# Landmark attention and the norm behind it in one stage, in a two-layer decoder on one core

## The reference, cut to what matters

```python
x = x + landmark(layernorm(x))            # L0_attn
x = x + heads(layernorm(x), ctx)          # L0_xattn: causal self and cross attention, 16 heads of 16
x = x + fp6_linear(layernorm(x))          # L0_ffn
x = x + hyperbolic(layernorm(x))          # L1_attn
x = x + two_mha_blocks(layernorm(x), ctx) # L1_xattn
x = x + experts(layernorm(x))             # L1_ffn, top 2 of 8

def landmark(x):                          # x: (4, 512, 256)
    q = softmax(x @ Wq + bq); k = softmax(x @ Wk + bk); v = x @ Wv + bv   # over all 256 features
    kl = k.reshape(B, 64, 8, 256).mean(axis=2)                            # 64 landmarks
    mid = (kl @ k.T) @ (k * v)                                            # (64, 256)
    return (q @ kl.T) @ mid
```

## Time and profile before

| | |
|---|---|
| median of 3 runs | 4048.33 us (4047.57 to 4056.62) |
| the profiled execution's own time | 4053.46 us |
| its span, first to last instruction | 4051.7 us |
| PE, DVE, ACT, POOL busy, share of the span | 83%, 51%, 40%, 23% |
| mean granted TensorE clock | 0.925 of full |

### The profile page before, as it was taken

How to read it: one execution, slowest core, us unless ns; L and a number is a source line. 1 busy time by engine, 2 the same in 40 slices (tenths; PEclk the granted TensorE clock), 3 DMA queues, 4 the chain that set the end, 5 groups by cost and what they waited for, 6 DMA issues and landing times. The chain is left out here.

```text
span 4051.7 us, 56156 instructions
## 1 busy us (share of the span) xinstructions
PE 3359.0 (83%) x21550; PEld 1837.2 (45%) x21550; DVE 2079.9 (51%) x4231; ACT 1633.4 (40%) x2349; POOL 919.6 (23%) x961
## 2 busy tenths in 40 slices
PE   6887788988887788988887888988876888947997
PEld 4325545254334535254234543263254452436886
DVE  5655665634655665634746555535656556430111
ACT  3353833333445642433437542433538333411221
POOL 1202822011105522012116420012018220140111
PEclk9998799999997898999997998999997999958998
DMA  4102012011202022011220121012120121134554
GB/s 116 55 13 78 1 45 89 20 38 45 59 24 55 1 49 84 20 43 40 59 69 11 32 71 51 19 24 60 38 78 1 45 72 37 35 126 159 172 180 150
DMA packets 227190, 239.73 MB, mean 59 GB/s; under 512 B 95542, under 2 KB 193956, under 8 KB 224612
## 3 DMA queue, kind: packets, MB, share of 16 engines
q1 hardware_dynamic: 219552, 215.73, 18.3%
q10 hardware_dynamic: 3620, 10.07, 0.7%
q0 software_dynamic: 3744, 10.26, 0.7%
HBM read 167.24 MB, written 68.76 MB: 58 GB/s over the span
## 5 line engine op out<-in xcount | busy, mean ns | idle before, releaser
L867 ACT ACTIVATE prob<-psum 128x1024 f32<-128x1024 f32 x384 | 372.2, 1021 | 509.0 <-PE psum L785 509.0
L1235 ACT ACTIVATE prob<-psum 128x1024 f32<-128x1024 f32 (+3 forms) x384 | 331.6, 914 | 363.8 <-PE psum L1136 363.8
L913 DVE TENSOR_REDUCE scr<-psum 128x1 f32<-128x512 f32 x576 | 369.0, 685 | 195.9 <-PE psum L772 192.1
L1275 DVE TENSOR_REDUCE stats<-psum 128x1 f32<-128x512 f32 (+3 forms) x576 | 331.9, 619 | 140.9 <-PE psum L1124 137.7
L782 PE MATMUL psum<-stack 32*128 32x512 f32 x1536 | 226.5, 660 | 15.2 <-ACT prob L867 10.4
L398 PE MATMUL psum<-ident 128*128 128x128 f32 x1704 | 213.5, 280 | 0.0
L398 PEld LDWEIGHTS psum<-ident 128*128 128x128 f32 x1704 | 203.7, 195 | 14.9 <-issue 13.8
L1124 PE MATMUL psum<-stack 96*128 96x512 bf16 (+3 forms) x576 | 181.8, 364 | 31.5 <-DVE stats L1275 31.1
L815 PE MATMUL psum<-prob,ones_f 128*32 128x512 f32 x1536 | 202.1, 594 | 0.0
L1151 PE MATMUL psum<-prob,vbig 128*32 128x512 f32 (+3 forms) x1536 | 189.4, 566 | 4.2 <-ACT prob L1235 4.2
L2832 PE MATMUL psum<-xgT,ew 128*128 128x256 f32 x736 | 167.8, 387 | 18.0 <-DVE xgT L2880 18.0
(11 more groups left out here) (483 smaller groups left out, 6495.9 us busy)
## 6 DMA issues: line engine op xcount, KB each, us to landing
ew<-in_L_ffn_W SPq DMA_DIRECT2D x46, 1024.0 KB, 7.8
stack<-q_terms SPq DMA_DIRECT2D x144, 128.0 KB, 2.5
w_mlp<-in_L_xattn_a_li_w SPq DMA_DIRECT2D x16, 1024.0 KB, 6.2
q_terms<-parts SPq DMA_DIRECT2D x96, 128.0 KB, 2.2
stack<-k_terms SPq DMA_DIRECT2D x72, 128.0 KB, 2.9
stack<-k_terms SPq DMA_DIRECT2D x36, 256.0 KB, 4.4
w_mlp<-a_terms SPq DMA_DIRECT2D x36, 256.0 KB, 4.7
a_keys<-stack SPq DMA_DIRECT2D x4, 2048.0 KB, 6.3
```

The costliest lines, as they stand in the source:

```text
L867: act.activation(prob[:, i % 4, :, :], psum[:, 2 * p:2 * p + 2, :], ACT.Exp, scale=scale).then_inc(exped, 1)
L913: dve.tensor_reduce(found[:, c:c + 1], ring(i), AX.X, ALU.max).then_inc(freed, 1)
L1235: act.activation(prob[:, i % 4, :, q0:T], psum[:, 2 * p:2 * p + 2, q0:T], ACT.Exp, scale=scale).then_inc(exped, 1)
L1275: dve.tensor_reduce(found[:, c:c + 1], ring(i)[:, 0:keys_of(t)], AX.X, ALU.max).then_inc(freed, 1)
```

## The change

Four things are edited:

1. **Stores.** The stores of u2 count on a semaphore `rows_out` of the kernel instead of one of the stage, and nobody waits for them in u2. SP waits for them in the next batch's front (and, after the loop, in a small stage named "after"). PE runs four idle matmuls at the end of u2.
2. **Context norm.** The transposes of the normed context and ACT's write of `cnT` move from the end of front into Asm, behind the last products. PE runs four idle matmuls at the end of front.
3. **Asm by halves.** Maxima, exponentials, and divisions are done for tiles 0 and 1, then 2 and 3. Six keys are made ahead of the transposes, one behind the landmarks and one behind `mid`; k2 comes before k1.
4. **n2 gone.** The late values and the norm, by halves, are in Asm.

```diff
@@ mlp_unit, SP
                 for t in range(QT):
                     sp.wait_ge(done, t + 1)
-                    storing(sp, t).then_inc(stored, 16)
-                sp.wait_ge(stored, 16 * QT)
+                    storing(sp, t).then_inc(e.rows_out, 16)
@@ mlp_unit, PE, at the end when final is None
+                e.keep_running(pe, 4, 0)
@@ beginning
+        @block.sync
+        def _(sp):
+            sp.wait_ge(e.rows_out, 16 * QT)
...
-            pe.wait_ge(raw_in, 1)
-            pe.wait_ge(cn_made, CT)
-            for t in range(CT):
-                last = pe.transpose(psum[:, 6 + t // 4, t % 4 * P:(t % 4 + 1) * P], cn[:, t, :], ident[:, :])
-            last.then_inc(cn_turned, 1)
+            e.keep_running(pe, 4, 1)
...
-            act.wait_ge(cn_turned, 1)
-            act.activation(cnT.rearrange("p k (a n) -> p (k a) n", n=BANK), psum[:, 6:8, :], ACT.Identity,
-                           bias=affine[1][:, 0:1], scale=affine[0][:, 0:1])
@@ landmark_attention, DVE
+            for h in range(2):
+                for t in HALVES[h]:
+                    ins = dve.tensor_reduce(mxq[:, 2 * t:2 * t + 2],
...
+            take_key(0)
+            divide(0)
+            take_key(1)
+            divide(1)
+            take_key(4)
+            take_key(5)
+            dve.wait_ge(lm, 1)
+            dve.tensor_copy(klT, psum[:, 7, 0:KT * L].rearrange("p (k n) -> p k n", k=KT)).then_inc(lm_in, 1)
             dve.wait_ge(soft, QT)
...
+            join(0)
+            join(1)
+            variance(0)
+            join(2)
+            join(3)
+            variance(1)
+            normalise(0)
+            normalise(1)
@@ landmark_attention, ACT, behind the exponentials of each half
+            take_key(2)
+            take_key(3)
+            copy_turned(0)
+            copy_turned(1)
+            take_key(6)
+            act.wait_ge(k1, 1)
+            act.copy(k1T, psum[0:L, 0, 0:T]).then_inc(k1_in, 1)
+            take_key(7)
+            act.wait_ge(cn_turned, 1)
+            act.activation(e.cnT.rearrange("p k (a n) -> p (k a) n", n=BANK), psum[:, 6:8, :], ACT.Identity,
+                           bias=affine[1][:, 0:1], scale=affine[0][:, 0:1])
+            for a in range(2):
+                act.wait_ge(valued, a + 1)
...
             for h in range(2):
+                act.wait_ge(x_turned, h + 1)
+                act.copy(xT[:, :, h * N:(h + 1) * N], psum[:, h, :].rearrange("p (k n) -> p k n", k=KT))
@@ landmark_attention, PE
             last.then_inc(lm, 1)
+            key(6)
...
-            for k in range(KT):
-                pe.matmul(psum[0:L, 6, :], klT[:, k, :], qAT[:, k, :], start=(k == 0), stop=(k == KT - 1))
             for t in range(QT):
                 for k in range(KT):
                     last = pe.matmul(psum[:, 5, t * L:(t + 1) * L], kAT[:, k, t * P:(t + 1) * P], klT[:, k, :],
                                      start=(t == 0 and k == 0), stop=(k == KT - 1), skip_group_check=True)
             last.then_inc(k2, 1)
+            for k in range(KT):
+                last = pe.matmul(psum[0:L, 0, :], klT[:, k, :], qAT[:, k, :], start=(k == 0), stop=(k == KT - 1))
+            last.then_inc(k1, 1)
...
             last.then_inc(md, 1)
+            key(7)
             pe.wait_ge(md_in, 1)
             pe.wait_ge(k1_in, 1)
             for t in range(QT):
+                if t == 1:
+                    pe.wait_ge(keys_by_act, 4)
                 pe.matmul(psum[:, t, 0:C], k1T[:, t * P:(t + 1) * P], mid, start=True, stop=True).then_inc(fin, 1)
+            pe.wait_ge(keys_by_act, 3)
+            for t in range(CT):
+                last = pe.transpose(psum[:, 6 + t // 4, t % 4 * P:(t % 4 + 1) * P], e.normed_context[:, t, :], ident[:, :])
+            last.then_inc(cn_turned, 1)
+            pe.wait_ge(e.loads, 16 * e.n_late)
...
+            pe.wait_ge(added, QT)
+            e.keep_running(pe, 3, 3)
+            for h in range(2):
+                pe.wait_ge(normed, 2 * h + 2)
...
+                last.then_inc(x_turned, 1)
+            e.keep_running(pe, 4, 3)
```

More of the change, by code:

```diff
@@ L1379, in _ @@
             sp.wait_ge(rows_in, 32)
+            sp.wait_ge(rows_out, 16 * QT)
 def batch(e, b):
@@ L1919, in _, with take_key @@
[L1919 to L1924 removed]
+            def take_key(i):
+                dve.wait_ge(keyed, i + 1)
+                dve.tensor_scalar(key_part(i), psum[:, KEY_BANK[i], :], key_bias(i), None, ALU.add).then_inc(keys_by_dve, 1)
@@ new lines, in divide, with join @@
+            def divide(h):
+                dve.wait_ge(exped, 4 * h + 4)
+                s = slice(4 * h, 4 * h + 4)
+                then(dve.reciprocal(sums[:, s], sums[:, s]))
+                for t in HALVES[h]:
+                    for i in range(2):
+                        ins = dve.tensor_scalar(half(t, i), half(t, i), sums[:, 2 * t + i:2 * t + i + 1], None, ALU.mult)
+                    ins.then_inc(soft, 1)
+            def join(t):
+                dve.wait_ge(fin, t + 1)
+                dve.tensor_tensor(x[:, t, :], psum[:, t, 0:C], x[:, t, :], ALU.add).then_inc(added, 1)
@@ new lines, in variance, with normalise @@
+            def variance(h):
+                for t in HALVES[h]:
+                    dve.wait_ge(added, t + 1)
+                    last = dve.bn_stats(stats[:, t, :], x[:, t, :])
+                then(last)
+                for t in HALVES[h]:
+                    last = dve.bn_aggr(mv[:, t, :], stats[:, t, :])
+                then(last)
+                s = slice(2 * h, 2 * h + 2)
+                dve.tensor_scalar(eps_var[:, s], mv[:, s, 1], EPS, None, ALU.add).then_inc(var_ready, 1)
+            def normalise(h):
+                dve.wait_ge(rstd_ready, h + 1)
+                for t in HALVES[h]:
+                    dve.tensor_scalar(xh[:, t, :], x[:, t, :], mv[:, t, 0:1], rstd[:, t:t + 1],
+                                      ALU.subtract, ALU.mult).then_inc(normed, 1)
@@ L2022, in take_late_values @@
-    def take_late_values(act, summed):
-        for a in range(ready):
-            act.wait_ge(summed, a + 1)
-            for i in range(2):
-                act.copy(Vc[:, CT - 2 * ready + 2 * a + i, :].rearrange("p (h w) -> p h w", w=W)[:, :, 0:D16],
-                         psum[:, 4 + a, i * C:(i + 1) * C].rearrange("p (h w) -> p h w", w=D16))
-    e.norm("n2", x, e.xh, turns=[(xT, None, None)], idle=(8, 5), beside=(late_values, take_late_values))
+    work, stack, colQK = e.work, e.stack, e.colQK
```

133 lines of the change are left out of this document (67 added, 66 removed).

## The result

The changed kernel takes **4009.29 us** (median of 4 runs, 4004.74 to 4015.05), the kernel before beside it 4052.47 us (4 runs, 4047.57 to 4057.63). The ratio is 0.9895, with a 95% interval of 0.988 to 0.991: faster by 1.05%. Beside each other the medians differ by 43.2 us. The profiled execution spans 4012.9 us, 38.8 less than that of before; the forecast's sum was 29.1.

A forecast was written before the change was run, and what follows sets the result against it. Bound: the chains across engines and barriers in some 55 us per batch, not PE's busy share. Savings of 5.8 + 5.6 + 16.2 + 1.5 = 29.1 us off the 4048.33 median gave 4019, range 4006 to 4031.

The forecast's parts named there:

- A: Batch's end: without SP's wait for the stores, 1.45 us saved in each of 4 batches, 5.8 us in all.
- B: End of front: without the context's transposes and write, Asm starts 1.4 us earlier per batch, 5.6 us in all.
- D: Front of three batches: a shorter idle gap of PE may keep its clock up; 1.5 us taken, bounds 0 and 4.4.
- C: Asm and n2, done by halves and merged: 16.2 us saved, 11.0 up to the first transposes and 5.2 behind them.
- Head: Stage start (S) to first transpose of q and k (T): 5.7 us, or 7.0 with half-clock keys; saves 11.0.
- Middle: From the first transpose of q and k (T) to the last products: T + 10.9, against T + 11.02 before.
- Tail: Adds, norm and barrier to the start of Ba: T + 19.85, T being the first transpose of q and k.
- the case of 4022: POOL's second power stands back until DVE has normed half 0: 3.1 us lost, sum about 26; chance 0.1.
- The clock stays up: Rival: PE's clock holds in front and the merged stage, 35.6 us saved, 4013; chance 0.14.
- The clock decides against it: Rival: half-clock keys in all batches, nothing gained in front's clock, 23.2 or 20 us saved, 4025 to 4028; chance 0.14.
- ACT becomes the tail: Rival: ACT, with 12.9 us of work in the merged stage, ends 2 us late, 8 us lost, 4027; chance 0.06.
- The change doesn't do what it says at the batch's end: Rival: branch and fetch, not the store, hold the loop; A and D are 0, 4026.5; chance 0.07.

The follow-up runs named there:

- e7: The kernel before with the edit of the stores alone (SP waits for them in the next batch's front), no idle matmuls: 4035.98 us, ratio 0.9973.
- e3: The changed kernel, but SP waits for the stores in u2 again: 4008.66 us, ratio 0.9889.
- e9: The kernel before with 64 more waits in POOL's program ahead of the loop, which shift its code, loop unedited: 4041.55 us, ratio 0.9978.
- e5: The changed kernel with the context norm's transposes and ACT's write back at the end of front, whose four idle matmuls are gone: 4011.56 us, ratio 0.9916.
- e4: The changed kernel, but DVE's first division waits for all eight exponentials, so the halves do not overlap: 4027.06 us, ratio 0.9942.
- e2: The changed kernel without the idle matmuls at the end of u2 and of front: 4002.4 us, ratio 0.9864.
- e8: The changed kernel with two idle matmuls instead of four at the end of front: 4003.25 us, ratio 0.9886.
- e12: The changed kernel without idle matmuls at the end of u2 and front and around the merged stage's transposes of x: 4005.09 us, ratio 0.989.
- e1: The kernel before with only the change's eight idle matmuls added, four at the end of u2 and four of front: 4039.32 us, ratio 0.9975.
- e11: The changed kernel with n2 a stage of its own again and no idle matmuls at the end of u2 and front: 4023.8 us, ratio 0.9957.

## Why the prediction was right, and by what part of it not

- **A, 5.8 us forecast, 4.6 measured** (3.5 in three gaps; the 1.1 behind the last batch I count in, though no row parts it from the experts). No wait of SP for the stores is left, but front's first transpose comes 2.50 us behind the last issue, not 2.2. The mechanism held and the size was off by a fifth. Alone the edit took 0.8 us off each gap (e7), and undone it cost 1.55 (e3); why these differ is open. e3 shows that in the changed kernel this piece can't be seen in the total.
- **B and D, 5.6 and 1.5 us forecast, 11.9 measured.** The step that failed is D: "behind 4.62 us of idle PE" I read the long fronts as lost clock. e9 takes 5.9 us off the fronts of before with the idle PE left as it is. What remains to the changed kernel, 76.5 to 70.5, is 6.0. Of it 4.9 is B, forecast at 5.6: from DVE's last part to S it takes 2.81 us in e9 and 1.58 after, in each batch. The other 1.1 stands ahead of DVE's first part, where PE ran less at half clock, and that is all that is left for D. The term put at nothing was POOL's late start in the earlier trace rows, in plain view: the power starts at 903.83, when DVE has been at the second half's statistics since 902.89. It makes 3.2 us of the 5.9; the rest is, for the most part, that PE ran less at half clock behind it.
- **C, 16.2 us forecast, 22.4 measured.** Head: T was S + 5.50 in all batches. I had 5.7 for two and 7.0 for two; all fast is 14.4 instead of 11.0. e5 shows what the 7.0 hangs on, the 2.4 us that PE stood idle for ACT's write: the piece that B removed. I had given B and the clock separate terms though one caused the other. Middle, forecast at T + 10.9: 10.87; batch 3 of before lost another 1.65 there at half clock. Tail, 19.85 forecast: 19.90. I had taken the tail of batch 1 for all batches; in batch 0 of before it was 1.3 us longer, because the late values of n2 ran at half clock behind 1.26 us of idle PE (1.97 us in batch 1):

```profile
66.16 3.65 PE L2018 MATMUL psum<-wBcv,c_pair 128*128 128x256 f32 x8 [1.26 <-PEq L69]
```

  So the head gave 3.4 us more than its 11.0, and middle and tail together some 2.8 more than the 5.2.
- **POOL's power, held back or not.** The row was right in the main: the power did not stand back, and the case of 4022 fell with it. It took 0.79 us beside DVE's norming; with DVE idle such a power takes 0.70 to 0.71 (2673.68 in the kernel before). The row's 1.52 us hid the same: 0.71 for the first power and 0.84 for the second. The Trainium skill, page "GPSIMD Engine Reference", section "1. Specifications", says that GpSimd contends with VectorE when that runs in a two-port mode or reads two SBUF inputs. The trace agrees in kind, but shows no wait for the whole of DVE's work: 0.09 to 0.13 us here, and 0.17 where another norm's power takes 0.87 beside DVE's `scalar_tensor_tensor`, which reads two SBUF tiles (517.85 in the kernel before).
- **Rivals.** "The clock stays up" (4013) is what happened in the merged stage. "The clock decides against it" did not, but e4 and e5 show it to be real: one wait of 2 us put back brings it in three or four of four batches. That all heads came out fast, where I had given half of them the slow clock, was not forecast but only allowed for. "ACT becomes the tail" is out: its late values end at 942.66, T + 16.7, half a us ahead of its next copy. "The change doesn't do what it says at the batch's end" is out by the gap.

The sum closes: 6.2 more from C and 4.8 more from B and D, 1.2 less from A, 2.4 more elsewhere, 2.6 less at the start: 9.6, which is 38.7 - 29.1. I don't explain the last two; they are as large as the spread of unedited stretches. So the range held in part by its width: it took in the 3.2 us of POOL's lateness, which the forecast had at nothing, and the good end of the clock.

**The best version** by median and ratio is e2, the changed kernel without the idle matmuls at the end of u2 and of front: 4002.4 us, 0.9864. e8 has 4003.25 (0.9886) and e12 4005.09 (0.989). None is told apart from the changed kernel's 4009.29 (0.9895), since the intervals overlap. By the stages e2 is the one to keep, for e12 pays with half clock in Ba.

## What to carry to other kernels

Read each engine's first instruction behind a loop's branch against the end of its input: a late start that nothing releases can be code being loaded, it moves with edits elsewhere, and padding ahead of the loop and the packets of the instruction queues test it. When a chain is shortened, look at where PE waits in it, for a wait of 2 us can cost a second time in the matmuls behind it, and here that second price was larger than the first. Before idle matmuls are taken out, look at the clock of the stage behind them, and not at the total alone. And cut in halves where PE would else wait for the whole.

## What the runs showed of the hardware that I had not expected

- POOL and PE can start up to 1.9 and 3.5 us late behind a loop's branch, in each iteration but the first, with all inputs there; 64 waits (POOL) or 32 matmuls (PE) ahead of the loop removed it in the profiled executions. PE's late starts came 1.57 to 1.59 us behind the landing of a 16.4 KB packet of code.
- 2.07 us of idle PE inside a stage led to 6.6 us lost in the next 17.5, at granted clock 0.61, in three of four batches; 1.16 us ahead of the keys never led to half clock, nor did 1.50 to 1.77 (e1, e2, e11, e12), while 1.26 us ahead of the late values did in batch 0 of the kernel before, and 1.45 us ahead of Ba in three of four batches of e12. So the length of the idle time alone doesn't decide it.
- A barrier with the loop's branch costs 2.5 us from the last issue to the first matmul, the barrier behind front 1.16, that ahead of Ba 0.8.
